# Two attention stages re-ordered: one run of eight head groups, projection per group, norms beside heads

## The reference, cut to what matters

```
x += 0.5 * ffn0(norm(x)); x += attn0(norm(x)); x += 0.5 * ffn0(norm(x))
x += 0.5 * ffn1(norm(x)); x += attn1(norm(x)); x += 0.5 * ffn1(norm(x))
attn: y = softmax(causal(q k^T / sqrt(32))) v per head (16 heads of 32);  return y @ Wo (+ bo in attn0)
```

## Time and profile before

| | us |
|---|---|
| median of 3 runs (2772.65 to 2775.14) | 2774.87 |
| the profiled execution's own time | 2772.28 |
| its span | 2770.5 |
| PE busy | 2638.7 (95%) |
| PE weight loads busy | 1996.1 (72%) |
| DVE / ACT / POOL busy | 1339.3 / 1085.3 / 637.9 |

### The profile page before, as it was taken

How to read it: one execution, slowest core, us unless ns; L and a number is a source line. 1 busy time by engine, 2 the same in 40 slices (tenths; PEclk the granted TensorE clock), 3 DMA queues, 4 the chain that set the end, 5 groups by cost and what they waited for, 6 DMA issues and landing times.

```text
span 2770.5 us, 35782 instructions
## 1 busy us (share of the span) xinstructions
PE 2638.7 (95%) x13216; PEld 1996.1 (72%) x13216; DVE 1339.3 (48%) x2712; ACT 1085.3 (39%) x1994; POOL 637.9 (23%) x1105
## 2 busy tenths in 40 slices
PE   6999789998999999999999999999999999999999
PEld 4788655475557888888888887655865578888887
DVE  7777655555646444533333345554455453333333
ACT  7554345635564223411212133556355641112111
POOL 3333511331223234411111111223122331111110
PEclk9999989999999999999999999999999999999999
DMA  4222021111111110000000002231223200000001
GB/s 141 69 70 71 29 63 35 51 41 38 36 55 50 35 42 8 23 31 23 23 23 25 30 8 62 67 77 55 51 60 73 55 31 24 23 23 23 31 16 61
DMA packets 60654, 121.63 MB, mean 44 GB/s; under 512 B 11840, under 2 KB 12864, under 8 KB 60480
## 3 DMA queue, kind: packets, MB, share of 16 engines
q1 hardware_dynamic: 60480, 119.35, 15.1%
HBM read 63.73 MB, written 13.63 MB: 28 GB/s over the span
## 4 chain that ended last, share of the span: by engine, by line
PE 76%; DVE 5%; issue 4%; ACT 2%; SPq 2%; DMA 1%; POOL 1%; DVEq 0%; ACTq 0%; POOLq 0%
PE psum L752 58%; PE psum L872 7%; PE psum L837 6%; PE psum L854 4%; SPq L1433 1%; PE psum L761 1%; DVE s1a0masked L1239 1%; ACT s4a1e L1051 1%; DVE s4a1masked L1239 1%; DVE tmp L1211 1%; PE psum L892 1%; PE psum L844 0%; POOL x L1347 0%; ACT s1a0qs L1004 0%; DVE s4a1y L1265 0%
## 5 line engine op out<-in xcount | busy, mean ns | idle before, releaser
L752 PE MATMUL psum<-hA_hi,wmem 128*128 128x256 f32 (+1 forms) x1536 | 404.9, 337 | 9.5 <-DVE tmp L1211 5.0
L752 PEld LDWEIGHTS psum<-hA_hi,wmem 128*128 128x128 f32 x1536 | 269.2, 191 | 47.3 <-DVE s1a0negmax L1239 7.5
L752 PE MATMUL psum<-hA_lo,wmem 128*128 128x512 f32 (+1 forms) x864 | 293.7, 340 | 0.0
L1239 DVE CUSTOM_DVE_ANT_0 s4a1masked<-psum,mask_q 128x640 bf16<-128x640 f32 (+7 forms) x256 | 188.7, 755 | 142.1 <-PE psum L837 89.4
L1239 DVE CUSTOM_DVE_ANT_0 s1a0masked<-psum,mask_q 128x640 bf16<-128x640 f32 (+7 forms) x256 | 188.3, 755 | 127.3 <-PE psum L837 74.5
L1051 ACT ACTIVATE s1a0e<-psum,p_scale 128x384 f32<-128x384 f32 (+5 forms) x384 | 203.9, 589 | 111.5 <-PE psum L854 109.3
L1051 ACT ACTIVATE s4a1e<-psum,p_scale 128x384 f32<-128x384 f32 (+5 forms) x384 | 204.3, 589 | 91.7 <-PE psum L854 90.2
L1178 DVE SCALAR_TENSOR_TENSOR x<-psum,x 128x512 f32<-128x512 f32 x256 | 175.5, 688 | 86.3 <-PE psum L752 82.4
L1149 DVE TENSOR_TENSOR s5f1prod<-psum,s5f1silu 128x512 f32<-128x512 f32 x64 | 44.2, 691 | 298.8 <-PE psum L752 298.8
L1149 DVE TENSOR_TENSOR s3f1prod<-psum,s3f1silu 128x512 f32<-128x512 f32 x64 | 44.2, 691 | 294.1 <-PE psum L752 294.1
L752 PE MATMUL psum<-s3f1w,s3f1a 128*128 128x512 f32 x768 | 181.0, 391 | 0.9 <-POOL s3f1w L1337 0.9
(11 more groups left out here) (208 smaller groups left out, 5010.9 us busy)
## 6 DMA issues: line engine op xcount, KB each, us to landing
s1a0qst<-s1a0qs SPq DMA_DIRECT2D x96, 128.0 KB
s4a1qst<-s4a1qs SPq DMA_DIRECT2D x96, 128.0 KB
s4a1kst<-s4a1ks SPq DMA_DIRECT2D x96, 128.0 KB, 2.3
raw<-in_gate SPq DMA_DIRECT2D x44, 256.0 KB, 2.7
raw<-in_up SPq DMA_DIRECT2D x44, 256.0 KB, 2.7
raw<-in_down SPq DMA_DIRECT2D x44, 256.0 KB, 2.8
rounded<-s0f0w SPq DMA_DIRECT2D x24, 256.0 KB, 2.0
s2f0w<-rounded SPq DMA_DIRECT2D x24, 256.0 KB, 5.1
```

The costliest lines, as they stand in the source:

```text
L752: ins = pe.matmul(out_, w, m, start=n == 0, stop=n == len(terms) - 1)
L1239: dve.tensor_tensor_reduce(T[s]["masked"][b][turn % 2][:, 0:width].rearrange("p (z w) -> p z w", **bare), scores, mask_q[:, SEQ - width:SE ...
```

## The change

- `HEADS_ALL` = 32 heads in eight groups run in one loop of 256 units; group g belongs to batch g // 4. The rows of head 16 follow those of head 15, and nothing drains between the batches. There are one `e32`, `masked`, `ysb` and one copy of the v weights (before: one for each batch).
- The pieces of group 4 (q and k, batch 1), its v products (from unit 125 in a0, 124 in a1) and weights become jobs beside the heads. The pieces of a group alternate q and k (before: all q, then all k).
- `y` holds one group. After a group's last head, two `y_tp` (4 transposes each) turn it, and eight `oproj` of 3 matmuls each add this group's share to x, one per unit, beside the next group's heads. `oproj` takes one of the six banks that all steps share.
- In group 2 the norms of batch 1, in group 6 those of the next stage's first half run beside the heads, one tile every 3 units from unit 15. In a0 the `bias_x` steps run one per unit from unit 1 of groups 0 and 4.
- The o weights are loaded per group, one piece of 512 columns at unit 25, into buffers of their own.
- The clears and the q stack's fourth DMA are gone. The row matmul reads 96 partitions, the key matmul 98 (before: 128 both). A POOL memset of 2 rows x 4096 writes the ones.
- The DMA scratch of the compiler's setting is 2048 bytes, which leaves room for the buffers.

```
+        for g in range(GROUPS_ALL):
+            at, b = g * UNITS, g // HPG
+            if g + 1 < GROUPS_ALL:
+                put(group_jobs(g + 1), at + 2 * ((g + 1) % HPG == 0), 2)
+            if g + 2 < GROUPS_ALL:
+                put(group_weights(s, g + 2), at + 20, 2)
+            put([split(s, "o", g, 0)], at + 25, 0)
+            if g % HPG == 2:
+                c = 0 if b else 2
+                last_norm.update({(s + b, c): [], (s + b, c + 1): []})
+                put([[[("ln_stats", s + b, t)], [], [("ln_norm", s + b, t)], [],
+                      [("ln_tp", s + b, t)], [("ln_lo", s + b, t)]]
+                     for t in range(c * CT, (c + 2) * CT)], at + 15, 3)
+            if grouped and g % HPG == 0:
+                put([[[("bias_x", s, b, t)]] for t in range(ST)], at + 1, 1)
+        last = (GROUPS_ALL - 1) * UNITS
+        jobs = first_weights(s + 1)
+        put(jobs, last + 2, (UNITS - 4) // len(jobs))
+        put(values(1), HEADS * ST - 3, 3)        # a0;  a1: HEADS * ST - 4, 1
 ...
+            if jt == ST - 1:
+                job = [[], [("take", s, n)], [], [], [("y_turn", s, n)], [("y_fin", s, n)]]
+                g, j = divmod(n, HPG)
+                if j == HPG - 1:
+                    job += [[("y_tp", s, g, 0)], [("y_tp", s, g, 1)]]
+                    job += [[("oproj", s, g, t)] for t in range(ST)]
+                side.start(job)
 ...
         elif kind in ("ln_tp", "piece", "v_tile", "v_chunk", "v_turn", "row", "m_tp", "key",
-                      "y_turn", "y_tp") or kind == "down" and step[4] >= 2:
+                      "y_turn", "y_tp", "oproj") or kind == "down" and step[4] >= 2:
 ...
-                    ins = pe.matmul(ps[:, z, 0:pw], q_st[:, j, i * P:(i + 1) * P],
+                    ins = pe.matmul(ps[:, z, 0:pw], q_st[0:STACK, j, i * P:(i + 1) * P],
 ...
-                products(ps[:, 0, :], [(yt[yp][:, k, t % 2, :], o_w[wp][k]) for k in range(KT)
-                                       for wp, yp in THREE], sem["o_proj"])
+                products(ps[:, 0, :], [(yt[yp][:, t, :], o_w[wp][:]) for wp, yp in THREE],
+                         sem["o_proj"])
```

More of the change, by code:

```diff
@@ L188, in attention @@
         plan.append(("v_ones", s))
[L189 to L217, removed]
-            if grouped:
[L220 to L296, removed]
@@ new lines, in attention, with group_jobs, row_unit @@
+        plan.append(("k_ones", s))
+        v_weights = Beside(plan)
+        v_weights.waiting += [split(s, "v", 0, k) for k in range(1 if grouped else KT)]
+        def group_jobs(g):
+            return [[[("piece", s, g, n, i)], [("piece_out", s, g, n, i)]]
+                    for i in range(4) for n in names_of_group(s, g)]
+        def row_unit(u):
+            n, i = divmod(u, ST)
+            if n < HEADS_ALL:
+                plan.append(("row", s, n, (u - AHEAD) % ST))
+                if i == ST - 1:
+                    side.start([[], [("m_tp", s, n)], [("m_lo", s, n)]])
@@ new lines, in values @@
+        def values(b):
+            if grouped:
+                return [[[("v_chunk", s, b, c)], [("v_turn", s, b, c)], [("v_out", s, b, c)]]
+                        for c in range(2)]
+            return [[[("v_tile", s, b, t)], [("v_out", s, b, t)]] for t in range(ST)]
+        first = Beside(plan)
+        first.waiting += group_jobs(0)
+        while first.waiting or first.running:
+            first.tick()
+            v_weights.tick()
+        v_weights.flush()
+        for j in range(HPG):
+            for n in "qk":
+                plan.append(("stack", s, 0, n, j))
@@ new lines, in attention, with put @@
+        side = Beside(plan)
+        side.waiting += values(0)
+        tiles, wait = len(side.waiting), 2
+        for u in range(-wait, AHEAD):
+            side.tick((u + wait) * tiles // (AHEAD + wait)
+                      - (u + wait - 1) * tiles // (AHEAD + wait))
+            if u >= 0:
+                row_unit(u)
+        side.flush()
+        beside = defaultdict(list)
+        def put(jobs, first, step):
+            for k, job in enumerate(jobs):
+                beside[first + step * k].append(job)
@@ new lines, in attention @@
+        for u in range(HEADS_ALL * ST):
+            n, i = divmod(u, ST)
+            g, at = divmod(u, UNITS)
+            side.tick(0)
+            row_unit(u + AHEAD)
+            for z in range(1 if SEQ - i * P <= CH else 2):
+                plan.append(("key", s, n, i, z))
+            plan.append(("e_mask", s, n, i))
+            behind.append((n, i))
+            if len(behind) > PV_LAG and i % 2 == 1:
+                times_v(*behind.pop(0))
+                times_v(*behind.pop(0))
+            for job in beside.pop(u, []):
+                side.start(job)
+            if g + 1 < GROUPS_ALL:
+                for j, when in enumerate((17, 18, 24, 31)):
+                    if at == when:
+                        for m in names_of_group(s, g + 1):
+                            plan.append(("stack", s, g + 1, m, j))
@@ L298, in make_plan @@
+        for unit in behind:
+            times_v(*unit)
+        side.flush()
     plan += [("x_in", t) for t in range(CT)]
@@ L399, in strip_turns @@
     for step in plan:
-        if step[0] != "key" or step[5] > 0:
+        if step[0] != "key" or step[4] > 0:
             continue
-        unit = step[1:5]
-        key = step[1:3]
-        width = SEQ - unit[3] * P
+        unit = step[1:4]
+        key = step[1]
+        width = SEQ - unit[2] * P
         begin = at[key] if at[key] + width <= size else 0
@@ L617, in w_read @@
                 return read + [(kept[GROUPS["f0"] - 2], 3 * PIECES * 16)] if p == 0 else read
-            if name == "v":
-                return [(sem["pv"], at("pv", "pv", s, 0, HEADS - 1, ST - 1))] if g else \
-                    [x_done(p, NT - 1)]
-            last = [("stack", s, g, n, HPG - 1 if n == "q" or STAGES[s] == "a1" else 0, j)
-                    for n in "qk" for j in range(HPG)]
-            return [stack_in(*step) for step in last]
+            if name == "o" and g:
+                return [(sem["o_proj"], at("o_proj", "oproj", s, g - 1, ST - 1))]
+            return [x_done(p, NT - 1)]
         def w_ready(s, name, g):
@@ L1217, in piece_out @@
                     return
-                stage_read(s, b, n, g)
+                for free in stage_read(s, n, g):
+                    on.wait_ge(*free)
                 on.wait_ge(sem["qk_hi"], at("qk_hi", *step))
```

400 lines of the change are left out of this document (185 added, 215 removed).

## The result

The changed kernel took 2857.52 us (median of 4 runs, 2855.51 to 2862.99), the kernel before beside it 2773.76 (2770.95 to 2775.14): a ratio of 1.0306, 95% interval 1.0289 to 1.0324. It is 84 us slower, where I had forecast 38 faster. The miss is 121.5 us. All rows of the kernel after come from its profiled execution, 2862.99 us, which is the slowest of the four.

The account below looks back on a forecast made before the run. PE was taken to bound the heads, so only stretches without heads could be gained: 36.0 us in a0 plus 21.3 in a1, together 57.3, less 18.0 taken off, leaving 39.3. Forecast median 2736 us, range 2708 to 2764.

Parts of the forecast that it names:

- The frame: Attention stages: PE sets the pace while heads run, so gains lie only in stretches where no head runs.
- Start 11.5: Start of a0: without the clears, head 0's first pv comes 11.5 us earlier, at 361.0 instead of 372.45.
- a1's 5.4: Start of a1: without the clears DVE's last piece is done 5.4 us earlier, with head 0 at 1712.2.
- Boundary: Between a0's batches, heads 15 to 16: the stretch without heads goes, giving 23 of a0's 36 us.
- The partitions: Rows and keys reading 96 or 98 partitions in 1536 matmuls: taken as 0, ends 11 us less or more.
- DVE keeps up; I take 0.05: Projection drains beside heads: 112 DVE additions at 0.05 us of PE time each, 5.6 us taken off the gain.
- The third rival: Projection's banks bind: PE waits one DVE addition per product beside heads, 77 us instead of 5.6, time 2807; chance 0.07.
- I take 0.6, since ACT catches up: Output-weight copies on ACT beside heads: 0.6 us for each of 14 pieces, 8.4 us taken off the gain.
- The second rival: Output weights hold ACT up in full: 14 x 2.0 = 28 us instead of 8.4, about 2757; chance 0.13.
- at nothing: Norm steps on POOL, ACT and DVE beside heads: no cost; if not hidden, some 16 additions of 0.8 us.
- My marker for the banks: Heads with projection: PE's waits for DVE's addition or row maxima growing to 40 us per stage would show banks bind.

Follow-up runs that it names:

- own_bank: The changed kernel with each output product taking the free one of pv's two banks instead of one of the six shared ones: 2890.33 us.
- o_gap: The changed kernel with ScalarE's copy of each output weight three units behind its DMA instead of one: 2837.15 us.
- proj_out: The changed kernel with y transposes, output products, their drains and output weights left out for six of eight groups per attention stage (output incomplete): 2717.49 us.
- norms_tail: The changed kernel with the next stage's eight norms put behind the last head instead of beside heads 26 to 31: 2891.08 us.
- all_three: The changed kernel with eight products in one block, seven banks in rotation (one for pv), and ScalarE's output-weight copy three units behind its DMA: 2761.05 us.

## Why the prediction was wrong

- **The frame held.** PE sets the pace while heads run, the feed-forward stages kept their length, and the heads' own pace is as it was. Start 11.5: 9.5 came (372.45 to 362.91). a1's 5.4: 3.3. Boundary: no stretch without heads. The partitions: nothing.
- **The step that failed first: "DVE keeps up; I take 0.05"** for the projection's drains. The measured excess is 5.3 us a group. Of its 74 in 14 groups I had 14 in the drains and o weights together; 60 are missed. I argued with DVE's load (57%, and 1.8 us of work in 2.1). The load is still that, and the wait is none of load: DVE stands for the product, PE stands for what DVE has behind it, at a lead of two units at most. Grouping the products gives back 51, a seventh bank 36, no additions 41. The third rival had the size, 0.69 for each product and 77. The Trainium skill, "Trainium Kernel Development and Optimization", section "Best Practices", says to mind PSUM pressure, and the seventh bank's 36 us agree. I gave this rival 0.07, because the same additions cost PE nothing between the batches. There a product is 2.80 long and nothing else asks for the banks; that row said nothing of heads. Its mechanism was at most half of it: products that no longer take one of the six banks (own_bank) were 33 slower, though there each waits for the addition before it.
- **The o weights**, "I take 0.6, since ACT catches up": ACT's waits came to 14.5 us in 11 places (3.7 in a0, 10.8 in a1), and o_gap gave 20, where I had 8.4. In a1 PE pays for the waits in full and more, 3 to 5 us a head, as the exponential behind the copy is late too (1.72 above). The second rival (28) was nearer, though its sign, 16 waits of 2 us or more, didn't come: three were that long.
- **The norms**, "at nothing" beyond four transposes: 50 instead of 11.6, so 39 missed, at least (28 of the 32 norms are in the 50, and in two of the four places group 4's weights too). A norm is 0.36 of PE, but it has two operations of 0.6 to 0.8 on ACT, two of 0.69 on DVE and a bank. I priced the engine that bounds, and not the chain that hangs between its instructions. What exactly makes it dear stays open: pairs and wider spacing made it 7 and 8 slower, but both also moved norms beside the products. To the stage's end they can't go either: there they cost 26 and 23 more.
- The sum, in the profiled executions, where the miss is 130.0 (2862.99 against 2733.0): 60 for projection and o weights, 39 for norms, 8 in starts and ends (the two starts gained 4.1 less than forecast, the two tails are 4.1 longer), and some 18 around heads 12 to 17 (pieces of the next batch, values and projection together, by proj_out's distances; not taken apart). That is 125 of 130; 5 stay open. Part of each is clock. The mean granted clock went from 0.991 to 0.982 of the span. Where PE sets the pace that is 2770.5 x 0.009 = 25 us lost before and 2861.3 x 0.018 = 52 after, so up to 27 of the miss were paid this way, behind small waits that my sum didn't have; the other three executions have 0.984 to 0.986 and less of it.
- My marker for the banks (PE's waits for the addition or row maxima "grow to 40 us per stage") was not reached and looked at the wrong waits. Those for the addition and for `negmax` and `mrow` went from 22 to 28 us in a0 and from 12 to 19 in a1. All waits for DVE while heads run went from 30 to 57 and from 19 to 44: the growth is in `y` and in the norms' `hA_lo`, which stand in DVE's queue among the rest. And the cost is spread over waits, longer products and clock; the distance of heads is the measure.

## What to carry to other kernels

A free share of an engine isn't room in its queue: a small step put between a pipeline's units costs a hand-over on each engine that it touches, here 5 us beyond the 6 us of work, until it is grouped (eight products in one place cost near their price) or the lead is longer. Price a moved step by all its instructions on all engines and by its banks, and take the price from a stretch where it stood in such company. Try the parts alone first: here the clears, a small part of the edit, gave all that the whole gave once it was mended.

## What the runs showed of the hardware

The granted clock gives small waits a second price. In norms_tail's end, by stretch:

```profile
860.00:915.00 55.00, 36.41 (x156) 25.50 (x156) 22.47 (x43) 20.96 (x35) 12.69 (x35) 0.72 0.15 54
```

PE stood 1.4 to 2.0 us between short bursts, and the clock went to its lower level (1.2 of 2.4 GHz). It was still there for the first 13 of the 24 dense matmuls behind, which so took 8.29 instead of 5.73 us. Two stretches among them, 6 and 11 matmuls in 2 us:

```profile
897.00:899.00 2.00, 2.00 (x6) 1.54 (x6) 0.93 (x2) 0.00 (x0) 0.00 (x0) 0.50 0.00 0
...
901.00:903.00 2.00, 2.00 (x11) 1.65 (x10) 1.90 (x4) 0.00 (x0) 0.00 (x0) 1.00 0.03 8
```

Over the whole span the clock was 0.982 in the changed kernel and 0.988 in all_three, where PE's waits in the heads are 39 and 38 us instead of 66 and 58.
